# Output product of a scan layer by halves of D, and the last four experts of a MoE summed on TensorE instead of through DRAM

## The chip, the cores and the metric

One NeuronCore of a Trainium2 chip runs the whole program in one launch. The metric is the device time of one execution in microseconds (us), and the median over runs is compared. The profile is one further execution, recorded by the hardware profiler.

## The reference, cut to what matters

A small vision tower on 64 images of 17 tokens (a class token and 16 patches), so 1088 tokens of width D = 256, in float32. With h the running state:

```python
h = tok(x)                                   # patch product, class token in front
h = h + L0_attn(layernorm(h))                # recurrent mixing over the 17 tokens
h = h + L0_ffn(layernorm(h))                 # 4-bit fake-quantised gate / up / down
h = h + L1_attn(layernorm(h))                # 16 heads, causal
h = h + L1_ffn(layernorm(h))                 # MoE, 64 experts, top 6, capacity 128

# L0_attn, the part that the change touches
out = A + exp(u + k_t) * (v_t * Bacc + c_t)           # two linear recurrences A and Bacc over t
A = exp(-w) * A + m_t * exp(k_t) * v_t
Bacc = exp(w) * Bacc + m_t / exp(k_t)
return (sigmoid(r) * out) @ Wo.T

# L1_ffn, the part that the change touches
y_e = (silu(x_e @ w1[e].T) * (x_e @ w3[e].T)) @ w2[e].T   # for each expert e, its up to 128 tokens
y = sum over the 6 experts of a token of y_e * weight
return y + shared(x)
```

## The kernel before, in words

The 1088 tokens are NT = 9 tiles of up to 128 rows (the last has 64). Each engine has its own instruction list, written out by hand, and semaphores are the only order between them: what an engine waits for is written in its list, and everything behind a wait waits too.

**The scan stage.** The channels lie on the partitions, in two halves o = 0, 1 of D. VectorE (DVE) runs per half a scan for Bacc and one for A (L1580, L1589) with the elementwise steps around them (L1584 to L1596). Then, for both halves, it multiplies the state by the sigmoid (L1599) and counts s_y0. TensorE (PE) waits for s_y0 = 2 and makes the output product of every token tile, with both halves of D accumulated in one PSUM bank (L803). It has six banks for this (2 to 7), so tiles 6 to 8 wait until tiles 0 to 2 have been added to h. DVE adds each tile to h (add_mixed, through the helper at L1425), between the steps that round the third weight matrix (L1473, L1477, L1481, L1503). ScalarE (ACT) squares each added tile (L1126), and DVE, GpSimd (POOL) and ACT build the next layernorm from that (L1444, L588, L1450 to L1454, L1134).

**The expert loop.** run_steps goes through steps n = -5 to 66. In step n, PE transposes the tokens of expert n+1 (L1064), makes its two first products for n (L1074), transposes the hidden values of n-1 (L1082) and makes the second product of n-2 in bank 5 or 7 by turns (L727 to L729, six matmuls of float32r, on high and low parts). ACT copies the result of n-3 to SBUF (L1386, s_yb), and POOL scatters it to the DRAM tensor y_rows by an indirect DMA (put, L687), one row for each token and each of its six choices. DVE has in each step the two low parts of w2 (L1871, L1894), the gated product (L1881), a small slot computation (L1885) and the low part of the hidden values (L1892). y_rows is zeroed at the start of the kernel.

**The end.** The sync engine (SP) waits for all 64 puts (L549) and then reads y_rows back by token tile, nine DMAs into picked (L551). The four odd tiles are summed on PE, with the identity as the stationary operand, six float32 products each (L1115), and DVE adds the sum (L1904). The five even tiles are summed on DVE with four additions each (L1908 to L1911). Every tile counts s_fin, and SP writes the output in three DMAs (L556).

Of the kernel before, what the change touches and what calls it, by code (L numbers as in the profile page):

```python
# [10 lines left out]
F32 = mybir.dt.float32  # L11
# [14 lines left out]
CH = 4  # L26
# [25 lines left out]
EB = 8  # L52
SG = CAP // EB
# [54 lines left out]
def build(nc, A, out):  # L108
    with ExitStack() as ctx:
# [148 lines left out]
        spread_e = reg2.cut([E, E, SG], BF16)  # L258
        code = reg2.cut([P, N])
# [15 lines left out]
        picked = reg2.cut([P, NT, TOPK * D])  # L275
        assert reg2.at <= high_at and 2 * DC * SI + DC * E <= 2 * 3 * DC * P
# [23 lines left out]
        shared_l = [cuts(shared_low, k * DC * SI, [DC, SI]) for k in range(2)]  # L300
        gate_l = cuts(at_word(R1 + gate_at, DC * E, "gate_low"), 0, [DC, E])
# [7 lines left out]
        w2_h = [cuts(high, k * 2 * D, [2, D])[0:EH] for k in range(2)]  # L309

# [21 lines left out]
        s_edec = sem("s_edec")  # L332
        s_msk = sem("s_msk")
        s_d0 = sem("s_d0")
        s_omu = sem("s_omu")
# [54 lines left out]
        s_shi = sem("s_shi")  # L390
        s_slo = sem("s_slo")
# [38 lines left out]
        s_best = sem("s_best")  # L430
# [4 lines left out]
        s_back = sems("s_back", 5)  # L435
        s_sum = sem("s_sum")
        s_fin = sem("s_fin")
# [17 lines left out]
        LN_PARTS = [(0, 6), (6, NT)]  # L455

# [12 lines left out]
        def _(sp):  # L469
# [78 lines left out]
            for j in range(4):  # L548
                sp.wait_ge(s_add[j], 16 * E // 4)  # L549
            for t in range(NT):  # L550
                sp.dma_start(picked[0:rows(t), t, :],  # L551
                             y_rows[1 + TOPK * P * t:1 + TOPK * (P * t + rows(t)), :].rearrange("(p k) d -> p (k d)", k=TOPK)
                             ).then_inc(s_back[t // 2], 16)
# [3 lines left out]
            sp.wait_ge(s_out, 48)  # L557

        @block.gpsimd
        def _(pool):  # L560
# [146 lines left out]
        def _(pe):  # L707
# [87 lines left out]
            transpose_weight(1)  # L795
            pe.wait_ge(s_y0, 2)
            for t in range(NT):
                if t < 6:
                    pe.wait_ge(s_rkv_ev, 24)
                else:  # L800
                    pe.wait_ge(s_h1, t - 5)
                for c in range(DC):
                    mm = nc.tensor.matmul(ps[0:rows(t), 2 + t % 6, 0:D], vv[:, c, t * P:t * P + rows(t)],  # L803
                                          rw[:, 3, c * D:(c + 1) * D], start=(c == 0), stop=(c == DC - 1))
                mm.then_inc(s_wo0, 1)
# [179 lines left out]
            pe.wait_ge(s_slo, 1)  # L985
# [70 lines left out]
            def pe_step(n, b, m8):  # L1056
# [28 lines left out]
                if 0 <= n - 2 < E:  # L1085
# [3 lines left out]
                    need(pe, s_yb, e - 1)  # L1089
                    for c in range(2):  # L1090
# [21 lines left out]
            for t in range(1, NT, 2):  # L1112
                pe.wait_ge(s_back[t // 2], 32)
                for k in range(TOPK):
                    mm = nc.tensor.matmul(ps[:, t // 2, 0:D], ident[:, :], picked[:, t, k * D:(k + 1) * D],  # L1115
                                          start=(k == 0), stop=(k == TOPK - 1))
                mm.then_inc(s_sum, 1)

        @block.scalar
        def _(act):  # L1120
# [35 lines left out]
            for t in range(NT):  # L1156
# [9 lines left out]
                if t == 4:  # L1166
                    act.wait_ge(s_rw, 16 * 5)
                    nc.scalar.activation(edec[:, 0, :], rvec[:, 3, :], ACT.Exp, scale=-1.0).then_inc(s_edec, 1)
                    nc.scalar.activation(edec[:, 1, :], rvec[:, 3, :], ACT.Exp).then_inc(s_edec, 1)
                    nc.scalar.activation(eu, rvec[:, 4, :], ACT.Exp).then_inc(s_edec, 1)  # L1170
                    act.wait_ge(s_edec, 3)
# [12 lines left out]
            act.wait_ge(s_omu, 1)  # L1184
            act.wait_ge(s_mixz, 3)
# [155 lines left out]
            for n in range(HP + 1):  # L1341
                if n == HP:
# [4 lines left out]
                    nc.scalar.activation(gate_h, gate_w, ACT.Copy).then_inc(s_shi, 1)  # L1347
# [620 lines left out]
```

## Time and profile before

| what | us |
|---|---|
| median of 3 runs | 670.97 |
| lowest, highest | 668.98, 674.72 |
| the profiled execution's own time | 670.08 |
| its span (first to last instruction) | 668.1 |

Over the span PE is busy for 532.0 us, DVE for 432.1, ACT for 359.1 and POOL for 224.2. Matmul spans overlap each other, so a busy PE is not a PE at its peak. The granted TensorE clock was 0.906 of full speed on average. A row of the profile has the start or the busy time, the line of the kernel, the engine, the operation, and the output and input by name. "region" is one of two large SBUF regions that many tensors share, "ps" is PSUM.

### The profile page before, as it was taken

How to read it: one execution, taken by the hardware profiler on the slowest of the kernel's cores; microseconds unless marked ns; L12 is line 12 of the kernel's file. 1: busy time of each engine (PE TensorE's matmuls, PEld its weight loads, DVE VectorE, ACT ScalarE, POOL GpSimd, SP SyncE). 2: the span in 40 equal slices, each digit the busy share in tenths (PEclk: the TensorE clock that was granted, in tenths of full speed). 3: DMA queues.
4: the chain of work that ended last, by engine and by line, in shares of the span. 5: the costliest groups of instructions: out<-in, count | busy, mean ns of one | idle time of the engine just before them, and what ended most of it. 6: DMA issues, size and time to landing. Idle time of an engine off the chain costs nothing.

```text
span 668.1 us, 9827 instructions
## 1 busy us (share of the span) xinstructions
PE 532.0 (80%) x3182; PEld 426.3 (64%) x3182; DVE 432.1 (65%) x982; ACT 359.1 (54%) x894; POOL 224.2 (34%) x234
## 2 busy tenths in 40 slices
PE   3959750465646999999999999999998889788845
PEld 3737640133325999999998878766666656556634
DVE  4987998999996355556547135756566656554526
ACT  1668614355445577787775456156555645565600
POOL 2010001034325111111112312466667667666510
PEclk9987966768756999999999999999989989998969
DMA  8960000046000000000000010146666657566466
GB/s 278 382 241 0 1 0 0 0 139 189 0 1 1 25 25 25 25 25 25 1 1 1 1 48 21 26 117 199 177 178 184 190 149 222 166 196 170 133 251 225
DMA packets 44054, 67.44 MB, mean 101 GB/s; under 512 B 11149, under 2 KB 27142, under 8 KB 43876
## 3 DMA queue, kind: packets, MB, share of 16 engines
q1 hardware_dynamic: 36836, 64.62, 30.8%
q0 software_dynamic: 7168, 2.20, 1.6%
q8 instruction: 26, 0.43, 0.3%
q14 instruction: 24, 0.20, 0.1%
HBM read 66.81 MB, written 17.72 MB: 127 GB/s over the span
## 4 chain that ended last, share of the span: by engine, by line
PE 44%; DVE 24%; issue 11%; POOL 6%; DMA 5%; ACT 5%; another core or an unknown queue 3%; SPq 1%; POOLq 0%; ACTq 0%; DVEq 0%
PE ps L729 5%; PE ps L727 5%; PE ps L938 5%; PE ps L728 5%; PE ps L896 4%; PE ps L927 4%; PE ps L1074 4%; POOL y_rows L687 3%; PE ps L734 3%; DMA region<-y_rows 2%; POOL region L678 2%; PE ps L910 2%; DVE region L1676 2%; PE ps L803 2%
## 5 line engine op out<-in xcount | busy, mean ns | idle before, releaser
L1074 PE MATMUL ps<-region 128*128 128x352 f32 x256 | 91.1, 480 | 6.6 <-issue 4.2
L687 POOL DMA_INDIRECT y_rows<-region x64 | 66.0, 1032 | 53.9 <-ACT region L1386 30.3
L1732 DVE TENSOR_TENSOR region<-ps,region 32x136 f32<-32x136 f32 x128 | 38.1, 297 | 60.2 <-PE ps L896 58.7
L678 POOL DMA_INDIRECT region<-x_rows,region x64 | 68.8, 1074 | 20.2 <-issue 18.0
L727 PE MATMUL ps<-nTh,high 128*128 128x272 f32 (+2 forms) x248 | 74.1, 299 | 0.4 <-ACT region L1316 0.4
L728 PE MATMUL ps<-nTl,high 128*128 128x272 f32 (+2 forms) x248 | 71.7, 289 | 0.0
L637 POOL COPY region<-region 32x544 f32<-32x544 f32 x32 | 26.4, 825 | 122.4 <-DVE region L1751 120.9
L1406 ACT ACTIVATE high<-region 88x512 fp32r<-88x512 f32 x64 | 40.4, 631 | 41.0 <-remote 23.9
L1074 PEld LDWEIGHTS ps<-region 128*128 128x128 f32 x256 | 44.8, 195 | 25.1 <-issue 7.8
L1881 DVE SCALAR_TENSOR_TENSOR region<-region,ps 128x176 f32<-128x176 f32 x64 | 25.4, 397 | 51.9 <-ACT region L1396 21.9
L729 PE MATMUL ps<-nTh,pairs_low 128*128 128x272 f32 x192 | 55.5, 289 | 0.0
L727 PEld LDWEIGHTS ps<-nTh,high 128*128 128x128 f32 (+2 forms) x248 | 46.3, 187 | 1.5 <-ACT region L1316 0.6
L728 PEld LDWEIGHTS ps<-nTl,high 128*128 128x128 f32 (+2 forms) x248 | 46.3, 187 | 0.1
L1335 ACT ACTIVATE region<-ps 64x136 f32<-64x136 f32 x128 | 35.6, 278 | 19.9 <-PE ps L927 18.0
L588 POOL TENSOR_TENSOR rstd<-veps,mhalf 128x6 f32<-128x6 f32 (+1 forms) x8 | 9.2, 1148 | 101.9 <-DVE veps L1444 101.9
L727 PE MATMUL ps<-high,pairs_low 88*128 88x256 f32 x128 | 41.9, 327 | 0.5 <-DVE pairs_low L1892 0.5
L616 POOL TENSOR_TENSOR region<-region 128x1024 f32<-128x1024 f32 x9 | 19.1, 2126 | 63.3 <-DVE region L1706 63.3
L1871 DVE TENSOR_TENSOR w_low<-region,high 88x256 fp32r<-88x256 f32 x64 | 26.8, 419 | 20.2 <-ACT high L1406 18.6
L1396 ACT ACTIVATE region<-ps 128x176 f32<-128x176 f32 x64 | 20.2, 315 | 32.7 <-PE ps L1074 20.6
L1082 PEld LDWEIGHTS ps<-ident,region 128*88 128x88 f32 x128 | 14.6, 125 | 35.2 <-DVE region L1881 15.8
L729 PEld LDWEIGHTS ps<-nTh,pairs_low 128*128 128x128 f32 x192 | 36.6, 191 | 0.0
L728 PE MATMUL ps<-w_low,pairs_low 88*128 88x256 f32 x128 | 36.5, 285 | 0.0
(250 smaller groups left out, 1408.1 us busy)
## 6 DMA issues: line engine op xcount, KB each, us to landing
region<-moe_w SPq DMA_DIRECT2D x64, 352.0 KB
region<-moe_w SPq DMA_DIRECT2D x64, 176.0 KB
y_rows<-zrow SPq DMA_DIRECT2D x1, 6528.0 KB, 25.9
region<-y_rows SPq DMA_DIRECT2D x8, 768.0 KB, 9.7
region<-wqkv SPq DMA_DIRECT2D x8, 384.0 KB, 3.0
region<-ffn_w SPq DMA_DIRECT2D x2, 1024.0 KB, 8.0
region<-patches SPq DMA_DIRECT2D x3, 384.0 KB, 8.3
region<-patches SPq DMA_DIRECT2D x1, 1152.0 KB, 10.7
```

Source lines behind the costliest of these rows:

```text
L678: nc.gpsimd.indirect_dma_start(out=xb[m8], out_offset=None, in_=x_rows, in_offset=bass.IndirectOffsetOnAxis(ap=sloti[:, at:at + 1], axis=0 ...
L687: nc.gpsimd.indirect_dma_start(out=y_rows, out_offset=bass.IndirectOffsetOnAxis(ap=sld[m8], axis=0), in_=yb[m], in_offset=None, bounds_che ...
L727: nc.tensor.matmul(out, parts_a[0], parts_b[0], start=first, stop=False)
L728: nc.tensor.matmul(out, parts_a[0], parts_b[1], start=False, stop=False)
L729: return nc.tensor.matmul(out, parts_a[1], parts_b[0], start=False, stop=last)
L896: mm = nc.tensor.matmul(ps[:, 4 + g // 2, (g % 2) * 2 * GW:(g % 2 + 1) * 2 * GW], qT[:, 4 * t:4 * t + 4, :].rearrange("p b t -> p (b t)"), ...
L938: mm = nc.tensor.matmul(ps[0:rows(t), 4 + t % 4, 0:D], attnT[:, c, t * P:t * P + rows(t)], wo1[:, c, :], start=(c == 0), stop=(c == HP - 1))
L1074: mm = nc.tensor.matmul(ps[:, 2 + m % 2, 0:2 * EI], xbT[m % 2][:, c, :], w13[m][:, c, :], start=(c == 0), stop=(c == DC - 1))
L1335: ins = nc.scalar.activation(dst.rearrange("p (k w) -> p k w", k=2), ps[f, g % 4, 0:4 * GW].rearrange("p (k h w) -> p k h w", k=2, h=2)[:, ...
L1406: nc.scalar.activation(w2_h[m % 2], w2[m], ACT.Copy).then_inc(s_w2h, 1)
L1732: last = V.tensor_tensor(sc[r, s0:s0 + 8, 0:T].rearrange("p (a b) t -> p a b t", a=4), ps[r, 4:8, 0:4 * GW].rearrange("p a (b h t) -> p a ...
L1871: V.tensor_tensor(w2_l[k][:, 0, :], w2[k][:, 0, :], w2_h[k % 2][:, 0, :].bitcast(F32), ALU.subtract).then_inc(s_w2l, 1)
```

## The change

**In the scan stage** the product with the sigmoid of half 0 moves into the scans of half 1. PE then makes the products of half 0 for tiles 0 to 7, each into its own bank (all eight banks; the two that the weight transposes use are waited for by s_wT = 4), waits for s_y0 = 2 and adds those of half 1. Tile 8 follows in bank 2, after tile 0 has been added to h.

**At the end** the puts of experts 60 to 63 are left out, and SP starts to read back when the 60 others have landed. For each of the four late experts DVE makes a 0/1 matrix `spot_e` [128 slots x 1088 tokens] in float32r by one compare, and splits the expert's result into a high part (ACT's copy) and a low part (DVE). PE sums the late experts for every token tile by two matmuls of float32r for each expert and tile (72 in all), into one bank per tile. For tiles 1, 3 and 5 the six read-back rows are added in the same bank, by the products with the identity. For tiles 0, 2, 4, 6, 7 and 8 DVE adds the read-back rows as before (four additions) and then the PE sum (a fifth). The output goes in five DMAs. The second products of experts 62 and 63 get one more wait, on s_late, which counts the compares and the low parts together. The first part of the late sums waits for s_yb = 64.

Some semaphores are merged to make room (s_edec into s_d0, s_omu into s_mixz, s_shi into s_whi, s_slo into s_wlo, s_best into the DVE chain).

```diff
+LATE = 4
-        picked = reg2.cut([P, NT, TOPK * D])
+        picked = [reg2.cut([P, TOPK * D]) for _ in range(NT - 1)]
+        picked.append(wo1.rearrange("p a b -> p (a b)")[:, 0:TOPK * D])
+        spot_e = [nTh[:, 0, :], nTh[:, 1, :], nTl[:, 0, :], nTl[:, 1, :]]
+        SUM_BANK = [0, 1, 2, 3, 4, 6, 5, 7, 0]
+        PE_TILES = (1, 3, 5)
+        MIX_BANK = [2, 3, 4, 5, 6, 7, 0, 1, 2]
...
             for j in range(4):
-                sp.wait_ge(s_add[j], 16 * E // 4)
+                sp.wait_ge(s_add[j], 16 * (E - LATE) // 4)
...
-            for c, (a, b) in enumerate(CHUNKS):
-                sp.wait_ge(s_fin, b)
+            for count, a, b in ((6, 0, 5), (6, 6, 7), (7, 7, 8), (8, 8, 9), (9, 5, 6)):
+                sp.wait_ge(s_fin, count)
                 sp.dma_start(token_rows(out, a, b), tiles(h, a, b)).then_inc(s_out, 16)
...
-                if 0 <= n - 3 < E:
+                if 0 <= n - 3 < E - LATE:
                     put(n - 3, (m8 - 3) % EB)
...
+            def state_product(t, c):
+                return nc.tensor.matmul(ps[0:rows(t), MIX_BANK[t], 0:D], vv[:, c, t * P:t * P + rows(t)],
+                                        rw[:, 3, c * D:(c + 1) * D], start=(c == 0), stop=(c == DC - 1))
+            pe.wait_ge(s_y0, 1)
+            pe.wait_ge(s_rkv_ev, 24)
+            for t in range(NT - 1):
+                if t == 6:
+                    pe.wait_ge(s_wT, 4)
+                state_product(t, 0)
             pe.wait_ge(s_y0, 2)
+            for t in range(NT - 1):
+                state_product(t, 1).then_inc(s_wo0, 1)
+            pe.wait_ge(s_h1, 1)
+            for c in range(DC):
+                mm = state_product(NT - 1, c)
+            mm.then_inc(s_wo0, 1)
...
                     need(pe, s_yb, e - 1)
+                    if e - 1 > E - LATE:
+                        pe.wait_ge(s_late, e - 1 - (E - LATE) + LATE)
...
             pe.wait_ge(s_yb, E)
             pe.wait_ge(s_h4, NT)
+            pe.wait_ge(s_late, LATE)
+            pe.wait_ge(s_ehl, E)
+            def late_sums(t, j, more):
+                for u in range(2):
+                    mm = nc.tensor.matmul(ps[0:rows(t), SUM_BANK[t], 0:D], spot_e[j][:, t * P:t * P + rows(t)],
+                                          y_parts[j][:, u, :], start=(j == 0 and u == 0),
+                                          stop=(j == LATE - 1 and u == 1 and not more))
+                return mm
+            def row_sums(t):
+                pe.wait_ge(s_back[t], 16)
+                for k in range(TOPK):
+                    mm = nc.tensor.matmul(ps[0:rows(t), SUM_BANK[t], 0:D], ident[0:rows(t), 0:rows(t)],
+                                          picked[t][0:rows(t), k * D:(k + 1) * D], start=False, stop=(k == TOPK - 1))
+                mm.then_inc(s_sum, 1)
+            for j in range(LATE - 1):
+                pe.wait_ge(s_late, LATE + j + 1)
+                for t in range(6):
+                    late_sums(t, j, t in PE_TILES)
+            pe.wait_ge(s_late, 2 * LATE)
+            for t in range(6):
+                late_sums(t, LATE - 1, t in PE_TILES).then_inc(s_sum, 1)
+            for t in range(6, NT):
+                if t == NT - 1:
+                    pe.wait_ge(s_fin, 1)
+                for j in range(LATE):
+                    mm = late_sums(t, j, t in PE_TILES)
+                mm.then_inc(s_sum, 1)
+            for t in PE_TILES:
+                row_sums(t)
...
+                    else:
+                        nc.scalar.activation(y_parts[e - E + LATE][:, 0, :], ps[:, 5 + 2 * (k % 2), 0:D],
+                                             ACT.Copy).then_inc(s_yb, 1)
...
+            def gated_state(o):
+                dve.wait_ge(s_rkv_ev, (5 + o) * CH)
+                V.tensor_tensor(vv[:, o, :], sA[o], sig[:, o, :], ALU.mult).then_inc(s_y0, 1)
             for o in range(DC):
...
+                if o == 1:
+                    gated_state(0)
                 after(done_b)
...
-            for o in range(DC):
-                dve.wait_ge(s_rkv_ev, (5 + o) * CH)
-                V.tensor_tensor(vv[:, o, :], sA[o], sig[:, o, :], ALU.mult).then_inc(s_y0, 1)
+            gated_state(1)
...
+                if 0 <= n - (E - 2) < LATE:
+                    j = n - (E - 2)
+                    dve.wait_ge(s_tab, E // EB)
+                    V.tensor_scalar(spot_e[j], code, slot_of(slotf, E - LATE + j), float(SKIP), ALU.add,
+                                    ALU.is_equal).then_inc(s_late, 1)
+                if E - LATE <= n - 3 < E:
+                    e, k = n - 3, (m - 3) % 4
+                    j = e - E + LATE
+                    dve.wait_ge(s_yb, e + 1)
+                    V.tensor_tensor(y_parts[j][:, 1, :], ps[:, 5 + 2 * (k % 2), 0:D], y_parts[j][:, 0, :].bitcast(F32),
+                                    ALU.subtract).then_inc(s_late, 1)
...
+            add_rows_of(0)
+            add_rows_of(2)
+            add_sums(0)
+            add_sums(2)
+            add_rows_of(4)
+            add_sums(4)
+            add_sums(1)
+            add_rows_of(6)
+            add_sums(6)
+            add_sums(3)
+            add_rows_of(7)
+            add_sums(7)
+            add_rows_of(8)
+            add_sums(8)
+            add_sums(5)
```

## Rows read from the trace of the kernel before

**Rows 1.** The chain of waits, 50 to 160 us: start, us, what

```profile
89.02 2.51 DVE region L1599 x2
91.57 10.08 PE ps L803 x36
```

**Rows 2.** Timeline, 75 to 150 us: start, us, engine, line, operation, idle before

```profile
80.42 1.13 DVE L1584 TENSOR_TENSOR region<-region 128x960 f32<-128x960 f32 x1
...
91.43 2.29 DVE L1473 SCALAR_TENSOR_TENSOR region<-region 128x2048 f32<-128x2048 bf16 x1
...
99.04 0.49 ACT L1126 ACTIVATE xn<-h,mom 128x256 f32<-128x256 f32 x1
...
99.10 0.42 DVE L1425 SCALAR_TENSOR_TENSOR h<-ps,h 128x256 f32<-128x256 f32 x1
...
102.02 0.16 DVE L1444 TENSOR_SCALAR veps<-mom 128x6 f32<-128x6 f32 x1
```

**Rows 3.** Busy time by stretch, scan stage: A:B, length, engines (x), PEclk, DMA, GB/s

```profile
80.00:85.00 5.00, 0.00 (x0) 0.00 (x0) 5.00 (x4) 2.43 (x3) 0.00 (x0) 0.68 0.00 0
...
94.00:96.00 2.00, 2.00 (x8) 1.65 (x7) 0.80 (x5) 0.74 (x3) 0.00 (x0) 0.64 0.00 0
```

**Rows 4.** The chain of waits from 640 us to the end

```profile
640.20 0.35 SPq L551
...
643.98 16.16 DMA region<-y_rows
...
660.19 2.87 PE ps L1115 x12
...
665.30 0.42 DVE h L1911
```

**Rows 5.** Timeline of POOL, 590 to 641 us: the puts of experts 59 and 63

```profile
631.01 0.98 POOL L687 DMA_INDIRECT y_rows<-region  x1 [1.33 <-ACT region L1386]
...
638.03 0.98 POOL L687 DMA_INDIRECT y_rows<-region  x1 [0.31 <-issue]
```

**Rows 6.** Timeline, 629 to 646 us: the last steps of the expert loop

```profile
632.25 0.41 DVE L1894 TENSOR_TENSOR w_low<-region,high 88x256 fp32r<-88x256 f32 x1
...
634.03 0.41 DVE L1892 TENSOR_TENSOR pairs_low<-ps,pairs_low 88x256 fp32r<-88x256 f32 x1
...
634.37 0.41 DVE L1894 TENSOR_TENSOR w_low<-region,high 88x256 fp32r<-88x256 f32 x1
...
634.88 0.36 PE L727 MATMUL ps<-high,pairs_low 88*128 88x256 f32 x1
...
636.53 0.28 PE L728 MATMUL ps<-w_low,pairs_low 88*128 88x256 f32 x1
...
637.00 0.28 PE L729 MATMUL ps<-high,pairs_low 88*128 88x256 f32 x1
637.32 0.38 ACT L1386 ACTIVATE region<-ps 128x256 f32<-128x256 f32 x1 [1.08 <-PE ps L729]
```

**Rows 7.** DVE groups, shapes kept apart: count, busy us, mean ns, idle before

```profile
L1815 DVE TENSOR_SCALAR region<-ps 64x1088 f32<-64x1088 f32 x1 | 1.3, 1283 | 0.1
...
L1806 DVE TENSOR_SCALAR region<-region 128x576 bf16<-128x576 f32 x1 | 0.8, 797 | 0.0
...
L1817 DVE TENSOR_SCALAR region<-region 64x1088 bf16<-64x1088 f32 x1 | 0.7, 718 | 0.0
```

**Rows 8.** Busy time by stretch around the end of the loop, columns as in rows 3

```profile
638.00:640.00 2.00, 0.00 (x0) 0.00 (x0) 0.00 (x0) 0.00 (x0) 0.98 (x1) 0.53 0.20 66
...
650.00:652.00 2.00, 2.00 (x6) 1.57 (x6) 0.00 (x0) 0.00 (x0) 0.00 (x0) 0.55 1.03 420
```

**Rows 9.** Timeline, 640 to 668 us: the sums of the read-back rows

```profile
646.47 0.96 DVE L1908 TENSOR_TENSOR region<-region 128x768 f32<-128x768 f32 x1 [10.23 <-DMA region<-y_rows]
...
646.58 7.99 PE L1115 MATMUL ps<-region,ident 128*128 128x256 f32 x24 [9.30 <-DMA region<-y_rows]
...
648.38 0.43 DVE L1911 TENSOR_TENSOR h<-h,region 128x256 f32<-128x256 f32 x1
```

More of the change, by code:

```diff
@@ L258, in build @@
         spread_e = reg2.cut([E, E, SG], BF16)
+        reg2.cut([P, 64])
+        code_at = reg2.at
         code = reg2.cut([P, N])
@@ L274, in build @@
         reg2.restart()
-        picked = reg2.cut([P, NT, TOPK * D])
-        assert reg2.at <= high_at and 2 * DC * SI + DC * E <= 2 * 3 * DC * P
+        picked = [reg2.cut([P, TOPK * D]) for _ in range(NT - 1)]
+        assert reg2.at <= code_at and TOPK * D <= HP * D
+        picked.append(wo1.rearrange("p a b -> p (a b)")[:, 0:TOPK * D])
+        assert 2 * DC * SI + DC * E <= 2 * 3 * DC * P
         early.close()
@@ L309, in build @@
         w2_h = [cuts(high, k * 2 * D, [2, D])[0:EH] for k in range(2)]
+        y_parts = [cuts(shared_low, 0, [2, D]), cuts(shared_low, 2 * D, [2, D]), cuts(pairs_low, 4 * 2 * CAP, [2, D]),
+                   cuts(high, 2 * 2 * D, [2, D])]
         x_rows = nc.dram_tensor("x_rows", (N, XW), F32, kind="Internal").ap()
@@ L429, in build @@
         s_val = sem("s_val")
-        s_best = sem("s_best")
         s_wide = sem("s_wide")
@@ L1111, in _ @@
             pe.wait_ge(s_h4, NT)
-            for t in range(1, NT, 2):
-                pe.wait_ge(s_back[t // 2], 32)
+            pe.wait_ge(s_late, LATE)
+            pe.wait_ge(s_ehl, E)
+            def late_sums(t, j, more):
+                mm = None
+                for u in range(2):
[5 more added lines that the diff above has]
+                pe.wait_ge(s_back[t], 16)
                 for k in range(TOPK):
-                    mm = nc.tensor.matmul(ps[:, t // 2, 0:D], ident[:, :], picked[:, t, k * D:(k + 1) * D],
-                                          start=(k == 0), stop=(k == TOPK - 1))
+                    mm = nc.tensor.matmul(ps[0:rows(t), SUM_BANK[t], 0:D], ident[0:rows(t), 0:rows(t)],
+                                          picked[t][0:rows(t), k * D:(k + 1) * D], start=False, stop=(k == TOPK - 1))
                 mm.then_inc(s_sum, 1)
+            for j in range(LATE - 1):
[13 more added lines that the diff above has]
+                row_sums(t)
         @block.scalar
@@ L1899, in _, with add_rows_of, add_sums @@
             run_steps(dve_step)
-            for t in range(NT):
+            def add_rows_of(t):
                 r = slice(0, rows(t))
-                if t % 2:
-                    dve.wait_ge(s_sum, t // 2 + 1)
-                    V.tensor_tensor(h[r, t, :], ps[r, t // 2, 0:D], h[r, t, :], ALU.add).then_inc(s_fin, 1)
-                else:
-                    dve.wait_ge(s_back[t // 2], 16 * min(2, NT - t))
-                    p = picked[r, t, :].rearrange("p (k d) -> p k d", k=TOPK)
-                    link(V.tensor_tensor(p[:, 0:3, :], p[:, 0:3, :], p[:, 3:6, :], ALU.add))
-                    link(V.tensor_tensor(p[:, 0, :], p[:, 0, :], p[:, 1, :], ALU.add))
-                    link(V.tensor_tensor(h[r, t, :], h[r, t, :], p[:, 2, :], ALU.add))
-                    V.tensor_tensor(h[r, t, :], h[r, t, :], p[:, 0, :], ALU.add).then_inc(s_fin, 1)
+                dve.wait_ge(s_back[t], 16)
+                p = picked[t][r, :].rearrange("p (k d) -> p k d", k=TOPK)
+                link(V.tensor_tensor(p[:, 0:3, :], p[:, 0:3, :], p[:, 3:6, :], ALU.add))
+                link(V.tensor_tensor(p[:, 0, :], p[:, 0, :], p[:, 1, :], ALU.add))
+                link(V.tensor_tensor(h[r, t, :], h[r, t, :], p[:, 2, :], ALU.add))
+                link(V.tensor_tensor(h[r, t, :], h[r, t, :], p[:, 0, :], ALU.add))
+            def add_sums(t):
+                r = slice(0, rows(t))
+                dve.wait_ge(s_sum, NT + 1 + PE_TILES.index(t) if t in PE_TILES else t + 1)
+                V.tensor_tensor(h[r, t, :], ps[r, SUM_BANK[t], 0:D], h[r, t, :], ALU.add).then_inc(s_fin, 1)
+            add_rows_of(0)
[13 more added lines that the diff above has]
+            add_sums(5)
 def kernel(**inputs):
```

59 lines of the change are left out of this document (24 added, 35 removed).

## The prediction

> **What bounds the kernel now.** I read the chain of waits over the whole span, then the timeline of the two places that the change touches. In the scan stage the chain runs on VectorE through both scans and the two products with the sigmoid, which end at 91.5 us, and then on TensorE for 10.08 us through the output products [rows 1]. TensorE stands in the stretch from 80 to 85, whose mean granted clock of 0.68 says that it went from 2.4 GHz (1.00) to 1.2 GHz (0.50) at about 81.8; it came back at about 95.4 (0.64 over the stretch from 94 to 96) [rows 3]. VectorE has little to do in that time: 2.29 us of rounding twice and nine additions of 0.42 us that start 0.35 apart, and it comes to the variance of the next layernorm at 102.02 [rows 2]. At the end, the sync engine starts the read-back at 640.20, after the last put has landed. The chain then lies on these DMAs until 660.14 and on the last six products and additions until 665.72 [rows 4]. The output's last transfer takes the span to 668.1, that is 2.4 us more.
>
> **Part 1, the scans.** Nothing is added on VectorE: the product of half 0 (1.25 us) moves from behind the second scan to before it, so the second product still ends at 91.5 [rows 1]. It can run at about 81.5, behind L1584 [rows 2], and TensorE starts eight products of half 0 at about 82.9. Its clock is low then [rows 3]. A float32 product of 256 columns costs 0.43 us at 2.4 GHz (six take 2.87 with about 0.3 for the end of the pipeline [rows 4]), and twice that, 0.85, at 1.2 GHz. Eight cost at most 6.8 us and end by 89.7, under the scans. Behind 91.5 there are eight products of half 1 and the two of tile 8. VectorE goes through its rounding until 93.8, adds tiles 0 and 1, rounds again until 96.8, and adds tiles 2 to 7 until 98.9. TensorE, even wholly at the low clock, has tile 1 by 93.6 and tile 7 by 98.7, so VectorE is the bound. Tile 8 waits for the addition of tile 0 (93.8 + 0.35), long past; TensorE has it at about 97 if the clock rises at 95.4 as before, and at 100.4 if not. VectorE is done at 99.3. The variance also needs ScalarE's squares of tiles 0 to 5, which come 0.49 apart behind the addition of tile 2 (97.2), so the last ends at 99.4 [rows 2]. The variance starts at 99.45 in place of 102.02: **2.5 us saved**. The bounds are 1.2 (low clock throughout) and 2.9 (additions alone). What is behind it (power on GpSimd, normalisation, token scales) is a chain on VectorE that nothing fixes in time, so the saving should stay. Merging semaphores costs nothing: the merged waits are met by instructions that had ended anyway.
>
> **Part 2, the read-back.** The put of expert 59 starts at 631.01, that of 63 at 638.03 [rows 5]. The read-back needs no more than the first, so it starts 7.0 us earlier, at 633.2, and since the transfer then takes as long as before, the last tile is there at 653.1 [rows 4]. The DMAs therefore leave the critical path. What takes their place is work: that of VectorE and TensorE, both behind the end of the expert loop.
>
> **Part 3, the end of the loop.** VectorE gets four compares over 1088 elements. The rows hold two neighbours, 0.72 us for the SBUF form of the same length (L1817) and 1.28 for the one that reads PSUM (L1815). A compare of 576 elements took 0.80 (L1806), which is the slower rate [rows 7]. I take 0.72, as operand place and length match, and keep 1.28. The Trainium skill ("VectorE: DVE Perf Modes", the perf-mode tier table) gives an SBUF tensor_scalar in float32 two elements per cycle. L1817 agrees and L1806 does not; by the rule alone the compares cost what I take.
>
> The other steps on VectorE start about 0.37 apart [rows 6]. From 632.66 (end of L1894): compare 633.4; four steps to 634.9; compare 635.6; low part of 60 at 636.0; three steps to 637.1; compare 637.8; low part of 61 at **638.1**. The new wait of expert 62's product counts compares and low parts together, and its fifth count is just that low part. So the product that started at 634.88 [rows 6] starts at 638.2. Behind it in TensorE's queue stand the product of 63 and all sums. The granted clock was at 0.53 from 638 to 640 [rows 8], after a stretch in which TensorE had worked with gaps, and here the gap of 3 us comes before, so I take both products at the low clock, 1.3 us each (six matmuls 0.12 apart in the rows at full clock [rows 6], doubled, less overlap). Product 62 ends at 639.5, 63 at 640.8, its copy (0.38 [rows 6]) at 641.2. TensorE starts the late sums at 641.3 and VectorE ends its last low part at 641.7; the corresponding moment before was 637.7, ScalarE's last copy [rows 6].
>
> **Part 4, the sums.** 72 matmuls at 0.115 are 8.3 us at full clock, and 18 products with the identity at 0.43 are 7.7. The low clock lasts at first: before, from the start of the dense products at 646.58 [rows 9] to about 651.8 (0.55 over the stretch from 650 to 652 [rows 8]), 5.2 us; in the scan stage from 91.57 to 95.4, 3.8 us [rows 1, 3]. I take 5, which costs 2.5 us of work. The first 36 matmuls end at 648.1, and the sum of tile 0 is there at 648.4. VectorE has added the read-back rows of tiles 0 and 2 by then (641.7 + 2 x 2.35 = 646.4, four additions taking 2.35 us [rows 9]), so it waits 2 us. It takes the sums of 0, 2 and, after the rows of 4, that of 4, until 652.0. Tile 1 is behind all late sums on TensorE: 654.9. VectorE waits 2.8 us for it. Then it has left: three sets of rows (7.0) and six sums at 0.43 (2.6), together 9.6: **664.4 against 665.72**. The last two output DMAs are as short as before, and I add nothing. Gain of the tail 1.3 us. Its bounds: a clock that rises after 3.8 us gives 1.9, one after 7 us 0.3, compares at 1.28 take 1.7 off, TensorE at full clock throughout gives 3.8.
>
> **The sum.** 670.08 (profiled execution) - 2.5 - 1.3 = 666.3. That execution was 0.9 below the median of the runs, so the median after should be **667.2**, 0.6% less. A measurement of this kernel tells about 1% from no change.
>
> **Rivals.**
> A. TensorE keeps the high clock at the end. For it: the gap is only about 3 us, and in the scan stage TensorE stood from before 80 until its clock fell at 81.8 [rows 3]. Against: it fell at 638 behind work with shorter gaps [rows 8]. The tail then gains 3.8, with the highest first part 2.9: 664.3. Chance 0.12.
> B. The compares run at one element per cycle, as L1806 did. The low part of 61 then ends at 639.8, and everything behind moves by 1.7: the tail loses 0.4. 670.97 - 2.5 + 0.4 = 668.9. Chance 0.17.
> C. Slower: the clock stays at 1.2 GHz through the late sums and the products with the identity, since short float32r matmuls with gaps between groups are what it fell on at 638. The late sums cost 16.6 and tile 1 comes at 663.2, tiles 3 and 5 at 5.1 each behind; VectorE ends at 674.7, 9.0 later than before. 670.97 - 2.5 + 9.0 = 677.5. It is slower than before as soon as the low clock lasts some 13 us instead of 5. Against: in both stretches above it rose within 5.3 us of dense work. Chance 0.05.
> D. The scan part doesn't pay: TensorE's second half stays at the low clock and is late for tile 8, or the saving is taken up by a stall in the feed-forward stage. With 0 to 1.2 from it: 668.5 to 669.7. Chance 0.10.
> The forecast has the remaining 0.56.
>
> **Numbers.** Range 663.5 to 671.0: from A with a run-to-run margin of 0.8 to B and D together (671 with nothing from the scans and the tail at -0.4). C is outside, and so are extremes of the others. Faster by over 1% needs less than 664.3: half of A and a little of the forecast, 0.11. Slower by over 1% is C and what I overlook, 0.06. The rest is 0.83.
>
> **What would show it.** The first matmul of the output products at about 83 and the variance at 99.4; the DMA chain gone from the end; compares at 0.72 and a gap on TensorE of some 3 us before the product of expert 62; the first late sum at 639 (641.3 less the 2.5 of the scans); VectorE waiting twice for sums, 2 and 2.8 us; last addition at 662. I am wrong if the read-back is late all the same, if compares take 1.3, if the product of 62 isn't held, or if the granted clock at the sums isn't low for about 5 us.

## The result, and the profile after

| | median, us | lowest, highest | runs |
|---|---|---|---|
| kernel before | 670.8 | 668.07, 678.73 | 20 |
| kernel after | 668.0 | 663.91, 672.70 | 20 |

The ratio of times is 0.9959, with a 95% interval of 0.9941 to 0.9978: the change gains 2.8 us (1.5 to 4.0). The forecast was 667.2 and its range 663.5 to 671.0. All ratios in this text leave out runs more than 1.5% above the fastest of the same kernel in their batch, which takes away seven of the 17 runs of the kernel before in the second batch of experiments and at most one of any kernel elsewhere, so the ratios of that batch stand nearer to 1 than its medians do.

The profiled execution of the new kernel took 672.7 us with a span of 671.0, which is longer than that of before (670.08, 668.1) and the longest of its 20 runs. So the two spans can't simply be subtracted. I cut each profile at five events that both kernels have: the first scan, the variance of the next layernorm, the gated product of expert 0, the gated product of expert 63, and the last addition on VectorE.

| stage, us | before | after | difference |
|---|---|---|---|
| first scan to variance | 40.81 | 38.13 | -2.68 |
| to the gated product of expert 0 | 337.25 | 337.19 | -0.06 |
| to the gated product of expert 63 (expert loop) | 194.38 | 201.08 | +6.70 |
| to the last addition (tail) | 32.07 | 29.72 | -2.35 |
| to the end of the span | 2.38 | 2.67 | +0.29 |

Both stages that the change touches are shorter. The expert loop, in which nothing but four compares at its very end was added, is 6.7 us longer; the experiments come back to it.

**The scan stage.** The timeline of the kernel after, 80 to 103 us, the rows that answer to [rows 1, 2] (start, us, engine, line):

```profile
83.81 5.14 PE L805 MATMUL ps<-region 128*128 128x256 f32 x16 [3.54 <-DVE region L1630]
...
92.57 6.42 PE L805 MATMUL ps<-region 128*128 128x256 f32 x20 [3.62 <-DVE region L1630]
...
100.34 0.17 DVE L1494 TENSOR_SCALAR veps<-mom 128x6 f32<-128x6 f32 x1
```

And the busy time by stretch, with the clock in the column behind the five engines [rows 3]:

```profile
80.00:85.00 5.00, 1.46 (x8) 1.10 (x6) 5.00 (x5) 3.43 (x3) 0.00 (x0) 0.83 0.00 0
...
92.00:94.00 2.00, 1.43 (x6) 1.24 (x7) 2.00 (x2) 0.00 (x0) 0.00 (x0) 0.89 0.00 0
94.00:96.00 2.00, 2.00 (x6) 1.63 (x5) 1.97 (x6) 0.78 (x3) 0.00 (x0) 0.50 0.00 0
96.00:98.00 2.00, 2.00 (x8) 1.36 (x7) 1.97 (x2) 0.31 (x2) 0.00 (x0) 0.76 0.00 0
```

The matmul records come in pairs for a float32 product, so x16 is eight products. Those of half 0 run from 83.8 to 89.0, under the scans. Behind the second product with the sigmoid stand 10 products for 18, in 6.42 us for 10.08. Behind it the clock was at 1.2 GHz (0.50) from about 93.6 (0.89 over the window from 92 to 94) to about 97 (0.76 over that from 96 to 98). It had been low once before, from 83.3 to 86.7, during the products of half 0.

**The tail.** The timeline of the kernel after, 637 to 669 us (the answers to [rows 4, 6, 9]):

```profile
637.47 0.78 DVE L1954 TENSOR_SCALAR nTh<-region 128x1088 fp32r<-128x1088 f32 x1
638.13 4.79 SPq L558 DMA_DIRECT2D region<-y_rows  x9
642.31 0.41 DVE L1960 TENSOR_TENSOR shared_low<-ps,shared_low 128x256 fp32r<-128x256 f32 x1
642.87 0.36 PE L734 MATMUL ps<-high,pairs_low 88*128 88x256 f32 x1 [3.00 <-DVE shared_low L1960]
646.05 4.82 PE L1136 MATMUL ps<-shared_low,nTh 128*128 128x256 f32 x24 [0.47 <-ACT high L1435]
652.64 0.83 DVE L1980 TENSOR_TENSOR h<-ps,h 128x256 f32<-128x256 f32 x2 [1.57 <-PE ps L1136]
656.39 7.93 PE L1145 MATMUL ps<-region,ident 128*128 128x256 f32 x36
659.18 0.42 DVE L1980 TENSOR_TENSOR h<-ps,h 128x256 f32<-128x256 f32 x1 [3.01 <-PE ps L1145]
667.58 0.75 DVE L1980 TENSOR_TENSOR h<-ps,h 64x256 f32<-64x256 f32 x2
```

The same stretch by windows (the answer to [rows 8]):

```profile
640.00:642.00 2.00, 0.00 (x0) 0.00 (x0) 2.00 (x6) 0.41 (x2) 0.00 (x0) 1.00 0.94 378
642.00:644.00 2.00, 1.13 (x6) 1.16 (x7) 1.42 (x3) 0.00 (x0) 0.00 (x0) 0.77 1.03 421
644.00:646.00 2.00, 1.58 (x8) 1.29 (x7) 0.42 (x1) 0.77 (x2) 0.00 (x0) 0.50 1.00 418
...
648.00:650.00 2.00, 2.00 (x11) 2.00 (x11) 1.90 (x4) 0.00 (x0) 0.00 (x0) 0.52 1.02 418
650.00:652.00 2.00, 2.00 (x19) 2.00 (x18) 1.01 (x3) 0.00 (x0) 0.00 (x0) 1.00 1.03 427
```

The read-back starts half a microsecond before the last gated product (638.61); before, it started 6.55 behind it (640.20, 633.65). VectorE waited 10.23 us for it then [rows 9] and has no wait for it now. In its place stand, in order, the hold of expert 62's product on TensorE (3.00 us, released by the low part of expert 61), a clock of 1.2 GHz from about 643 to 650, and two waits of VectorE for sums, 1.57 for tile 0 and 3.01 for tile 1.

### The profile page after: what moved, and what is told of

It reads as the page before. It is cut to its first block, busy times and chain, and to the rows that moved or that the text cites. A ratio compares the mean times of both kernels' runs of the same rounds, so it can differ in the third digit from the quotient of the medians.

```text
span 671.0 us, 9955 instructions
## 1 busy us (share of the span) xinstructions
PE 545.3 (81%) x3242; PEld 438.7 (65%) x3242; DVE 439.3 (65%) x995; ACT 358.8 (53%) x894; POOL 218.8 (33%) x230
## 4 chain that ended last, share of the span: by engine, by line
PE 56%; DVE 26%; ACT 6%; issue 5%; another core or an unknown queue 3%; DMA 1%; POOL 1%; SPq 0%; ACTq 0%; DVEq 0%
PE ps L1089 9%; PE ps L736 6%; PE ps L734 6%; PE ps L735 6%; PE ps L953 5%; PE ps L911 4%; PE ps L942 4%; PE ps L741 3%; PE ps L1097 2%; PE ps L925 2%; PE ps L1079 2%; DVE region L1731 2%; PE ps L1136 2%; DVE region L1742 1%
## 5 line engine op out<-in xcount | busy, mean ns | idle before, releaser
L1089 PE MATMUL ps<-region 128*128 128x352 f32 x256 | 93.0, 488 | 5.9 <-issue 3.1
L694 POOL DMA_INDIRECT y_rows<-region x60 | 62.2, 1037 | 58.1 <-ACT region L1433 39.1
L1089 PEld LDWEIGHTS ps<-region 128*128 128x128 f32 x256 | 45.7, 199 | 24.5 <-issue 7.3
L734 PE MATMUL ps<-high,pairs_low 88*128 88x256 f32 x128 | 43.0, 336 | 3.0 <-DVE shared_low L1960 3.0
L736 PE MATMUL ps<-high,pairs_low 88*128 88x256 f32 x128 | 37.7, 294 | 0.0
```

Source lines behind the costliest of these rows:

```text
L694: nc.gpsimd.indirect_dma_start(out=y_rows, out_offset=bass.IndirectOffsetOnAxis(ap=sld[m8], axis=0), in_=yb[m], in_offset=None, bounds_che ...
L734: nc.tensor.matmul(out, parts_a[0], parts_b[0], start=first, stop=False)
L736: return nc.tensor.matmul(out, parts_a[1], parts_b[0], start=False, stop=last)
L1089: mm = nc.tensor.matmul(ps[:, 2 + m % 2, 0:2 * EI], xbT[m % 2][:, c, :], w13[m][:, c, :], start=(c == 0), stop=(c == DC - 1))
```

## The experiments

Each ran with five rounds of timing. Kernels of one batch shared a chip and the runs of the kernel before: its median was 676.55 us in the first batch (the next four), 670.82 in the second, 675.67 in the third. A ratio is that of times to the kernel before in the same batch, and not exactly that of the two medians; the tail is the fourth stage of the table above.

**First batch: each part alone.** The scan part without the tail (read-back, puts and sums as in the kernel before):

```diff
+        MIX_BANK = [2, 3, 4, 5, 6, 7, 0, 1, 2]
...
+                if o == 1:
+                    gated_state(0)
...
+            for t in range(NT - 1):
+                state_product(t, 1).then_inc(s_wo0, 1)
```

> The scan part alone, the end as before. My theory: from the first scan to the variance of the next layernorm 2.7 us less than before (38.1 against 40.8 in the two profiles), and this stays as a constant shift up to the first expert. The median is 2.5 to 2.7 us lower than before (ratio 0.996), whatever the expert loop adds of its own from one execution to the next. Rival (a stall later takes it up): the shift at the first expert is under 1 us and the ratio is 1.000.

Measured: 673.53 us, ratio 0.9953 (0.9926 to 0.9979). Scan stage 38.12, tail 31.90.

The tail without the scan part, as an edit of the kernel after (the output products have both halves in one group again):

```diff
-                if o == 1:
-                    gated_state(0)
...
+            gated_state(0)
             gated_state(1)
```

> The end of the change alone, the scans as before. My theory: from the gated product of expert 63 to the last addition some 29.0 us, against 31.6 to 32.1 us before (the change as a whole had 29.4), so about 2 us or less are won there; the product of expert 62 is held about 3 us by the wait behind the compares, and tile 1's sum is late by 3 us for VectorE. Ratio 0.997 to 0.999. Rival (the tail gives nothing and the whole gain is that of the scans): ratio 1.000 and the same length of the tail as before.

Measured: 674.47 us, ratio 0.9965 (0.9943 to 0.9988). Scan stage 40.67, tail 30.77. Each part gains by itself, and neither leans on the other. The tail is 1.8 us longer than the 29 expected: the hold is 3.00 us as in the change, but the low clock lasted until 5.8 us into the late sums, and VectorE waited 2.43 us for tile 0 and 3.02 for tile 1.

**The four compares moved out of the end.** They need only the slot table (s_tab), which is complete long before the last steps:

```diff
-                if 0 <= n - (E - 2) < LATE:
-                    j = n - (E - 2)
+                if n in (50, 52, 54, 56):
+                    j = (n - 50) // 2
```

> The change, with the four compares moved to steps 50 to 56 of the expert loop, where VectorE waits a third of its time. The count for which the product of expert 62 waits is then that of the low part of expert 60. My theory (the compares and the wait that counts them hold the product of 62 and all sums behind it): no gap of 3 us on TensorE, the late sums start 3 to 3.6 us earlier relative to the gated product of expert 63, and the last addition comes 2 to 3.5 us earlier relative to it (26 to 27.5 us); the median is 2 to 3 us below the change. Rival (the read-back is the bound): VectorE waits for the rows of tile 2 or 4 instead and less than 1 us is won.

Measured: 665.62 us, ratio 0.9842 (0.9808 to 0.9875), tail 26.14. The timeline of this kernel:

```profile
634.39 0.36 PE L734 MATMUL ps<-high,pairs_low 88*128 88x256 f32 x1 [0.27 <-DVE shared_low L1960]
...
637.34 2.88 PE L1136 MATMUL ps<-shared_low,nTh 128*128 128x256 f32 x23 [0.47 <-ACT high L1435]
...
642.27 0.96 DVE L1971 TENSOR_TENSOR region<-region 128x768 f32<-128x768 f32 x1 [2.28 <-DMA region<-y_rows]
```

The hold of 3.00 us is 0.27. TensorE has no long gap, and in this profile its granted clock is 1.00 in every window from 634 to 642, and the late sums start 4.5 us behind the last gated product (632.85) instead of 7.4; 24 of them take some 3.0 us for 4.82. What VectorE then waits for is the read-back again, 2.28 us here and 0.56 and 0.83 further on.

**The gap kept, the clock held up.** Twelve bf16 products of 128x512 that nobody reads (the trace shows 11 records) stand on TensorE ahead of expert 62's wait, so it waits as long for VectorE but isn't idle:

```diff
+                    if e == E - 2:
+                        for i in range(12):
+                            nc.tensor.matmul(ps[:, 6, :], ident_bf[:, :], upto[:, 0:512], start=True, stop=True)
                     if e - 1 > E - LATE:
```

> The change, with twelve bf16 matmuls of 512 columns, whose result nothing reads, in the 3 us gap of TensorE before the product of expert 62. They add no data and end before the wait is met (12 x 0.215 = 2.6 us). My theory (the low granted clock at the start of the sums costs 2.5 us of work): the granted clock stays at 1.00 from the loop to the sums, the two products take 0.7 us each in place of 1.3, the 72 late matmuls 8.3 us in place of 10.5, and the last addition comes 2.5 to 3.5 us earlier relative to the gated product of expert 63. Rival (VectorE is the bound there anyway, or the clock falls all the same): under 1 us.

Measured: 668.27 us, ratio 0.9868 (0.9837 to 0.99), tail 26.93.

```profile
638.58 2.54 PE L1107 MATMUL ps<-upto,ident_bf 128*128 128x512 bf16 x11
641.38 0.39 PE L734 MATMUL ps<-high,pairs_low 88*128 88x256 f32 x1 [0.26 <-DVE shared_low L1963]
...
654.99 0.42 DVE L1983 TENSOR_TENSOR h<-ps,h 128x256 f32<-128x256 f32 x1 [2.54 <-PE ps L1148]
```

The product of 62 is as late as in the change (the compares are still there), but the clock stays at 1.00 from 638 to 646 and the tail is 2.8 us shorter than in the change's profile. This is the cost of the low clock by itself, from one profile of each kernel. The wait for tile 1 remains (2.54).

**Second batch: the change again, and its waits.** The change unaltered:

> The change itself once more, on the same chip as the three variants beside it. My theory: the three parts outside the expert loop repeat (scan stage to variance 38.1 us, from there to the first expert 337.2, tail from the gated product of expert 63 to the last addition 29 to 30), and only the expert loop differs from execution to execution (194 to 202 us so far, with the same instructions). So the ratio to before is 0.992 to 0.996. Rival (the change itself makes the loop longer, which had 201.1 us against 194.4 before): loops of 200 us and more again, and a ratio of 0.996 or higher.

Measured: 666.29 us, ratio 0.9970 (0.9932 to 1.0007); the medians of all runs, 666.29 and 670.82, give 0.9932. Scan stage 38.12, tail 30.66, with the same hold:

```profile
633.86 0.55 PE L734 MATMUL ps<-high,pairs_low 88*128 88x256 f32 x1 [3.00 <-DVE shared_low L1960]
...
644.57 0.83 DVE L1980 TENSOR_TENSOR h<-ps,h 128x256 f32<-128x256 f32 x2 [2.32 <-PE ps L1136]
...
651.11 0.43 DVE L1980 TENSOR_TENSOR h<-ps,h 128x256 f32<-128x256 f32 x1 [3.01 <-PE ps L1145]
```

```profile
632.00:634.00 2.00, 0.14 (x1) 0.17 (x1) 2.00 (x6) 0.00 (x0) 0.00 (x0) 0.62 1.00 415
```

The tail is 0.9 us longer than in the first profile of the same kernel. The hold is equal, but the clock fell at 632.5, inside it (0.62 over the window from 632 to 634), and was back only 5.5 us after the late sums began, for 3.9 in the first profile; the wait for tile 0 is 2.32 us for 1.57. The stage from the variance to expert 0, expected at 337.2, took 333.07 here: it varies from one execution to the next as the expert loop does (196.53 here).

The exact waits. The product of expert 62 overwrites the bank of expert 60, so it needs the low part of 60, which is the third count of s_late and not the fifth:

```diff
-                        pe.wait_ge(s_late, e - 1 - (E - LATE) + LATE)
+                        pe.wait_ge(s_late, 3 if e == E - 2 else 5)
```

> The change, with the two new waits at the count that is needed: third (low part of 60) for the product of expert 62, fifth (low part of 61) for that of 63, in place of fifth and sixth. The compares stay where they are. My theory (wait and compares hold the sums together): the product of 62 starts 2 us earlier, that of 63 and the sums 1.3 us earlier, and the gap of 3 us on TensorE is halved, so that the granted clock stays high in part of the executions: the tail is 1.3 us shorter where the clock falls (28 to 28.5) and up to 4 us where it doesn't. Rival (only the compares' time counts): under 0.5 us.

Measured: 662.42 us, ratio 0.9893 (0.9835 to 0.9952), tail 28.56.

```profile
631.82 0.36 PE L734 MATMUL ps<-high,pairs_low 88*128 88x256 f32 x1 [0.97 <-DVE shared_low L1960]
633.85 0.55 PE L734 MATMUL ps<-high,pairs_low 88*128 88x256 f32 x1 [1.08 <-DVE shared_low L1960]
```

The single gap of 3.00 us becomes two of about 1, and the clock falls all the same, at about 632.8, as the second of them begins. The windows of this kernel:

```profile
632.00:634.00 2.00, 0.92 (x7) 0.74 (x7) 2.00 (x6) 0.38 (x1) 0.00 (x0) 0.71 1.04 424
634.00:636.00 2.00, 1.53 (x7) 1.23 (x7) 0.81 (x3) 0.38 (x1) 0.00 (x0) 0.50 1.05 432
```

The late sums start 6.4 us behind the last gated product, for 7.6 in the change again and 7.4 in its first profile. So the merged count made them 1.1 to 1.3 us late, and the low clock was left. The tail is 2.1 us shorter than 30.66 and 1.2 shorter than 29.72; what of the 2.1 is not lateness goes with the clock, which was back 3.7 us after the late sums began instead of 5.5.

**TensorE's order of sums.** VectorE wants tile 1 before 6, 3 before 7; TensorE did all late sums first:

```diff
-            for t in range(6, NT):
-                ...
-            for t in PE_TILES:
-                row_sums(t)
...
+            row_sums(1)
+            late_all(6)
+            row_sums(3)
+            late_all(7)
+            late_all(8)
+            row_sums(5)
```

> The change, with TensorE's last work in another order: the read-back rows of tile 1 straight after the late sums of tiles 0 to 5, then tile 6, rows of 3, tiles 7 and 8, rows of 5; VectorE's order stays. My theory (tile 1's sum stands behind all late sums and VectorE waits 3 us for it): the wait is gone or under 0.5 us and the tail is 2.3 to 3 us shorter than that of the change on the same chip, about 27 us. Rival (the wait moves to another tile, 3 or 5, since TensorE's work in all is the bound): under 1 us.

Measured: 662.91 us, ratio 0.9887 (0.9829 to 0.9945), tail 28.57, 2.1 less than the change in the same batch.

```profile
654.09 0.42 DVE L1986 TENSOR_TENSOR h<-ps,h 128x256 f32<-128x256 f32 x1 [0.17 <-PE ps L1145]
```

The wait for tile 1 fell from 3.01 to 0.17. The tail won less than the 2.3 to 3 us expected, since VectorE waited 2.56 us for tile 0 (the low clock lasted until 6.1 us into the late sums) and 0.42 for tile 3.

**Both, and the read-back in the order of use.** Early compares, the order above, and the read-back as 0, 2, 4, 1, 6, 3, 7, 8, 5:

> Compares early (as in the run before), the order of the sums as in the run beside this one, and the tiles read back in the order in which they are used (0, 2, 4, 1, 6, 3, 7, 8, 5). With the compares early alone VectorE waited for rows of tiles 2, 4 and 6 (2.3, 0.6 and 0.8 us). My theory (then VectorE alone is the bound): no wait of VectorE over 0.7 us behind the last low part, tail 23 us (26.1 with the compares early alone), median 2.5 to 3.5 us below that run's, ratio to before 0.979 to 0.985. Rival (the read-back's rate is the bound whatever the order): tail 25.5 to 26.1.

Measured: 659.01 us, ratio 0.9846 (0.9788 to 0.9904), tail 27.13: longer than with the early compares alone (26.14), where less was expected. The timeline and a window of this kernel:

```profile
650.59 1.71 PE L1145 MATMUL ps<-region,ident 128*128 128x256 f32 x4 [2.19 <-DMA region<-y_rows]
651.67 3.46 PE L1145 MATMUL ps<-region,ident 128*128 128x256 f32 x9
...
655.17 0.42 DVE L1986 TENSOR_TENSOR h<-ps,h 128x256 f32<-128x256 f32 x1 [2.50 <-PE ps L1145]
```

```profile
652.00:654.00 2.00, 2.00 (x6) 1.55 (x6) 0.63 (x2) 0.00 (x0) 0.00 (x0) 0.50 0.07 19
```

I had moved tile 5 to the end of the read-back because it is used last, but it needs TensorE's six products after it lands, where an even tile needs only additions. TensorE stood 2.19 us for it, its clock fell, and the last products ran at 1.2 GHz with VectorE waiting.

**Third batch: mended, and the kernel before once more.** The same with the read-back as 0, 2, 1, 4, 3, 6, 5, 7, 8:

> The early compares and TensorE's new order, with the read-back in the order 0, 2, 1, 4, 3, 6, 5, 7, 8, so that no odd tile comes last. Theory: in the earlier kernel with the order 0, 2, 4, 1, 6, 3, 7, 8, 5 the last wait was for the rows of tile 5; with tile 5 seventh, TensorE's last six products start before 652 and VectorE ends its tail (last gated product to last addition) at 24.5 to 25.5 us, bound by its own additions and by the rows of tile 0 at the start. Time 0.980 to 0.985 of the kernel before. Rival: the transfers share the same queues, so that the order only moves the wait to the rows of tile 8, and the tail stays at 26 to 27 (ratio 0.984 to 0.988).

Measured: 666.27 us, ratio 0.9830 (0.9775 to 0.9885), tail 24.25. Its timeline:

```profile
640.49 4.64 PE L1136 MATMUL ps<-shared_low,nTh 128*128 128x256 f32 x24 [0.47 <-ACT high L1441]
...
646.90 0.83 DVE L1986 TENSOR_TENSOR h<-ps,h 128x256 f32<-128x256 f32 x2 [1.39 <-PE ps L1136]
...
650.60 0.43 DVE L1986 TENSOR_TENSOR h<-ps,h 128x256 f32<-128x256 f32 x1 [0.17 <-PE ps L1145]
```

No DMA wait of VectorE is left, and only that for tile 0 (1.39) is over half a microsecond. The rival, a wait for the rows of tile 8, did not occur, and the tail is just under the 24.5 expected. The clock fell here too, without a long gap: the first 24 late sums took 4.64 us where they took some 3.0 with the early compares alone.

The early compares and the order, with the read-back from 0 to 8:

> The early compares and TensorE's new order, the read-back in its original order 0 to 8. Theory: VectorE waits for the rows of tiles 2 and 4 as with the early compares alone, some 2.5 us, and for no sums; tail 25 to 26 us against 26.1 with the early compares alone, ratio 0.983 to 0.988. Rival: the order is worth 2 us here too, as it was in the change (28.6 for 30.7): tail 24.

Measured: 665.78 us, ratio 0.9833 (0.979 to 0.9877), tail 25.50, inside the range of the theory, but not by its waits. It had VectorE wait some 2.5 us for rows and for no sums; the profile has 1.27 and 0.27 us for rows and 0.86 for the sum of tile 0, and its clock was low from 641.3 to 648.1:

```profile
640.00:642.00 2.00, 1.40 (x10) 1.23 (x9) 1.42 (x4) 0.38 (x1) 0.00 (x0) 0.83 1.02 418
...
644.00:646.00 2.00, 2.00 (x11) 2.00 (x11) 1.62 (x4) 0.00 (x0) 0.00 (x0) 0.50 1.03 420
```

Each of the last two tails holds a wait for the sum of tile 0 that the low clock brought (0.86 us here, 1.39 above), so the 1.25 us between them is not the worth of the read-back order by itself. By time the two can't be told apart, since the intervals are 6 to 7 us wide, nor from the early compares alone (0.9842) or from the kernel with tile 5 last (0.9846). The four lie some 1.6% below the kernel before, and their intervals end below those of the change.

The kernel before, unchanged:

> The kernel before once more, unchanged, for the spread of one profiled execution against another: scan stage 40.8 us to within 0.1, tail 31.9 to 32.2, and the stage between them and the expert loop anywhere in 333 to 339 and 193 to 202, as in the kernels with the change. If instead the loop takes 194.4 to within 0.5 again, the 196 to 202 seen with the change are the change's doing. Ratio of times 1.000 within 0.005.

Measured: 678.18 us, ratio 1.0019 (0.9985 to 1.0053). Scan stage 41.08 (0.3 over the 40.8 expected), loop 202.02, tail 33.72. The window over the whole expert loop, of the kernel before in its first profile, of the kernel after, and of the kernel before in this run:

```profile
439.30:633.70 194.40, 173.14 (x919) 123.53 (x919) 116.72 (x359) 109.28 (x312) 124.77 (x119) 0.97 0.62 179
```

```profile
437.50:638.60 201.10, 177.55 (x918) 126.59 (x919) 116.93 (x356) 109.35 (x312) 123.86 (x118) 0.95 0.60 173
```

```profile
440.50:642.60 202.10, 176.56 (x919) 127.14 (x920) 116.92 (x359) 109.11 (x313) 123.72 (x119) 0.94 0.59 172
```

The same kernel took 194.4 us in one execution and 202.0 in another. VectorE's and ScalarE's work is the same to 0.3 us in all three; the mean granted clock is a little lower in the long ones, as cause or as effect. So the 6.7 us that the first profile showed against the change need no doing of it. The tail, expected at 31.9 to 32.2, was a miss: TensorE's last six products fell on the low clock (from 670.3 to 673.7 by the granted clock).

```profile
669.18 4.42 PE L1115 MATMUL ps<-region,ident 128*128 128x256 f32 x12 [1.94 <-DMA region<-y_rows]
...
673.64 0.42 DVE L1904 TENSOR_TENSOR h<-ps,h 128x256 f32<-128x256 f32 x1 [2.14 <-PE ps L1115]
```

In the first profile the same wait was 0.58 and the products took 2.87 [rows 4]. The kernel before thus has a tail of 32.07, 31.90 (the scan part alone) and 33.72, mean 32.56.

**All together.** If only the two touched stages count, a kernel gains 40.85 (the mean of the three profiles without the scan part) less its scan stage (38.12 where it has that part) and 32.56 less its tail. Against the measured ratios, as a share of the batch's median of before:

| kernel | tail, us | ratio by stages | ratio measured |
|---|---|---|---|
| scan part alone | 31.90 | 0.9950 | 0.9953 (0.9926 to 0.9979) |
| tail alone | 30.77 | 0.9971 | 0.9965 (0.9943 to 0.9988) |
| the change | 29.72, 30.66 | 0.9924 | 0.9959 (0.9941 to 0.9978), 0.9970 (0.9932 to 1.0007) |
| exact waits | 28.56 | 0.9900 | 0.9893 (0.9835 to 0.9952) |
| order of sums | 28.57 | 0.9900 | 0.9887 (0.9829 to 0.9945) |
| fillers in the gap | 26.93 | 0.9876 | 0.9868 (0.9837 to 0.99) |
| early compares | 26.14 | 0.9865 | 0.9842 (0.9808 to 0.9875) |
| early compares, order, read-back with tile 5 last | 27.13 | 0.9878 | 0.9846 (0.9788 to 0.9904) |
| early compares, order | 25.50 | 0.9855 | 0.9833 (0.979 to 0.9877) |
| the same, read-back 0, 2, 1, 4, 3, 6, 5, 7, 8 | 24.25 | 0.9837 | 0.9830 (0.9775 to 0.9885) |

The stages account for every kernel within its interval but one, which is a mild test, as the intervals are 3 to 8 us wide and each tail is that of one execution. The change, by its stages, should gain 5.1 us and gains 2.8 (1.5 to 4.0). Its two parts alone gained 3.2 and 2.4 by their ratios, 5.5 together, which agrees with the 5.1. In its second measurement the medians of all runs differ by 4.5 us (670.82 and 666.29), so the shortfall of 2.3 us rests mainly on the first. No stage that the profiles fix holds it: the two that the change doesn't touch vary more than that by themselves, from 333.1 to 338.5 and from 193.5 to 202.0. It stays open.

## Why the prediction was right, point by point

**The scans: right in mechanism and size.** Forecast 2.5 us, measured 2.68. Half 0 ran under the scans, VectorE and not TensorE was the bound behind 91.5, and the saving stood in all ten profiles that have the part (38.12 to 38.14). The whole stage began 1.0 us later in the profile after (first scan 62.21, before 61.21); with that taken off, the products of half 0 started at 82.8 for 82.9, and the variance at 99.34 for 99.45. Of TensorE's clock the working had another course. It took the clock as low when half 0 starts and as back at 95.4; with the products of half 0 under the scans it was low from 83.3 to 86.7, high again, and low once more from 93.6 to 97.0. That cost nothing, since VectorE did not wait for TensorE in this stage. The next stage kept the saving: the gated products of experts 0 to 10 came 1.7 to 2.3 us earlier in the profile after, which is at least 2.7 with that 1.0. Rival D is refuted: the stage paid in full, and the scan part alone took 3.2 us off the time (1.4 to 5.0).

**The read-back: right.** Off the chain in both profiles of the change. With the hold and the low clock gone it comes back as VectorE's waits of 2.28, 0.56 and 0.83 us, so it lay just under them.

**The compares: 0.78 us for 0.72.** Rival B (1.28) is refuted. The statement of the Trainium skill that the prediction set beside it ("VectorE: DVE Perf Modes", the perf-mode tier table, two elements per cycle for a float32 tensor_scalar in SBUF) agrees with the measured row.

**The hold of expert 62's product: right.** About 3 us were forecast, 3.00 measured, by the very instruction that was named, the low part of expert 61. From the last gated product to the first late sum the working gives 7.65 us (641.3 less 633.65), and the trace shows 7.44.

**The low clock: right in place and, on the mean, in size.** Products 62 and 63 ran 0.21 us apart for 0.12, and the first 24 late sums took 4.82. After the late sums began the clock was low for 3.9 us in the first profile, where I took 5; with the same hold of 3.00 us it was 5.5 in the change again, 5.8 in the tail alone and 6.1 with the other order of sums. The waits for tiles 0 and 1 were 1.57 and 3.01 us for 2 and 2.8, and 2.32 and 3.01 in the change again. Rival A (clock stays high) occurred in none of these four. The fillers priced it at 2.8 to 3.7 us, where the prediction had said 2.5: its bound of 3.8 for the tail's gain left the products 62 and 63 at their low-clock length of 1.3 us each, and the tail with fillers is 5.1 below 32.07. Rival C (clock low to the end) is refuted.

**The tail's gain: the new tail right, the old one taken from a single execution.** The forecast of 1.3 us is a tail of 30.75 us (664.4 less 633.65) against 32.07. Measured were 29.72 in the first profile, where the low clock was short, 30.66 in the second and 30.77 in the tail alone. The remaining work after tile 1 took 9.2 us for 9.6. What the step missed is on the other side: the 32.07 was taken as the kernel's own tail, though TensorE waits for rows there [rows 4] and its last products can meet the low clock, as they did once (33.72). One profiled execution was treated as the kernel. By the means of the table above the tail's gain is 2.4 us, of which half a microsecond hangs on that one execution of 33.72.

**The sum: near by luck.** 667.2 forecast and 668.0 measured, where the stages alone would give 665.7 (670.8 less 5.1). The forecast is nearer than its terms deserve: by those means the tail's term was too small by about 1 us, and a loss of some 2 us that no profile locates came against it.

## What to carry to other kernels

When work replaces a wait at the end of a kernel, look at what the new work sits behind: the four compares cost 3.1 us of VectorE at the one place where TensorE waited for it, and some ten steps earlier they cost nothing that shows; moving them took another 3.6 to 4.5 us off the tail, in a profile whose clock stayed high, beside the 5.1 us that the stages give the whole change. A semaphore that counts two kinds of events makes a wait for the later kind wait for both; write down which event each count is. And cut profiles into stages at events that both kernels have before any span is compared: here 7 us of spread in an untouched loop covered a gain of 3 to 11.

## What was not expected of the hardware

The expert loop took from 193.5 to 202.0 us in thirteen profiles, with the same instructions per step but for the compares. By batch, each on its own chip, it was 198.1 to 201.6, 193.5 to 197.0, and 198.6 to 202.0, and the medians of the kernel before went with it (676.55, 670.82, 675.67). Whether the chip or the execution sets it, these few profiles can't tell.

When TensorE's clock falls is not fixed by the gap at the end. In the profile after it stood at 1.00 for the whole gap of 3.00 us and fell at about 643.1, 0.2 us after work resumed. In the change again it fell at 632.5, 1.4 us before work resumed, and in the scan stage of the profile after at 83.3, half a microsecond before. Either way most of the price of a gap is paid behind it, in the low clock that lasts into the work. With the exact waits it fell as the second gap began, with one gap of 1 us ahead of it. The four kernels with early compares all have gaps of 0.3, 0.3 and 0.6 us up to the product of expert 63, and one more before the late sums. In the profiles of two of them the clock stayed at 1.00 through the first late sums (2.99 and 3.10 us for 24 of them), and in the other two it fell at 641.0 and 641.3 (4.64 and 5.36 us). So the early compares shorten the hold each time, and keep the clock up only in some executions. With the fillers of 2.5 us it stayed up in the one profile there is.
